# Value products of an attention kernel put into other slots, and transposes put ahead of scores

## The reference

```python
latent_kv = x @ w_kv_down                 # rank 128
kv = latent_kv @ w_kv_up
k, v = kv[..., :HD], kv[..., HD:]         # 16 heads of 64
q = (x @ w_q).reshape(Bx, Tx, N_HEAD, HEAD_SIZE)
att = einsum('bqhd,bkhd->bhqk', q, k) * HEAD_SIZE ** -0.5
att = softmax(where(causal, att, -inf))
y = einsum('bhqk,bkhd->bqhd', att, v).reshape(Bx, Tx, HD)
x = layernorm(x + y @ w_out)
x = layernorm(x + experts(x))             # router, top tokens per expert, gelu
```

## Time and profile before

| | us |
|---|---|
| median of 3 runs | 3311.64 (3307.95 to 3320.35) |
| profiled execution | 3316.82 |
| its span, first to last instruction | 3315.0 |
| busy in the span: TensorE | 2963.1 (89%) |
| VectorE | 2074.8 (63%) |
| ScalarE | 1933.2 (58%) |
| GpSimd | 1578.2 (48%) |

### The profile page before, as it was taken

How to read it: one execution, slowest core, us unless ns; L and a number is a source line. 1 busy time by engine, 2 the same in 40 slices (tenths; PEclk the granted TensorE clock), 3 DMA queues, 4 the chain that set the end, 5 groups by cost and what they waited for, 6 DMA issues and landing times. The chain is left out here.

```text
span 3315.0 us, 65032 instructions
## 1 busy us (share of the span) xinstructions
PE 2963.1 (89%) x20800; PEld 2263.0 (68%) x20800; DVE 2074.8 (63%) x5640; ACT 1933.2 (58%) x4173; POOL 1578.2 (48%) x1661
## 2 busy tenths in 40 slices
PE   7888888888888888888888888888999999999997
PEld 5555555555555555555555555558998999999996
DVE  5665666666666666666666666664596885544546
ACT  5666666666666666666666666664544444444443
POOL 3343334334334333433433343334776776666665
PEclk9999999999999999999999999999999999999998
DMA  2332333333333233233332423335754444443435
GB/s 69 108 109 89 110 106 94 111 104 106 95 101 121 87 101 117 91 115 99 104 104 92 129 84 113 108 106 214 271 209 118 107 122 101 89 113 87 86 72 157
DMA packets 342714, 374.37 MB, mean 113 GB/s; under 512 B 68296, under 2 KB 283080, under 8 KB 342368
## 3 DMA queue, kind: packets, MB, share of 16 engines
q1 hardware_dynamic: 300320, 319.62, 30.4%
q0 software_dynamic: 25152, 33.75, 6.1%
q10 hardware_dynamic: 16896, 16.78, 1.4%
HBM read 211.85 MB, written 158.16 MB: 112 GB/s over the span
## 5 line engine op out<-in xcount | busy, mean ns | idle before, releaser
L270 POOL TENSOR_SCALAR prob<-prob,inv 128x128 f32<-128x128 f32 (+7 forms) x1024 | 756.7, 750 | 1229.7 <-DVE inv L710 734.6
L705 DVE CUSTOM_DVE_ANT_0 s_ps<-s_ps,mask 128x128 f32<-128x128 f32 (+7 forms) x1024 | 757.0, 779 | 345.4 <-PE s_ps L411 338.6
L592 ACT ACTIVATE prob<-s_ps,neg_max 128x128 f32<-128x128 f32 (+7 forms) x1024 | 754.7, 740 | 282.3 <-DVE neg_max L705 278.6
L428 PE MATMUL t_ps<-ident,prob 128*128 128x128 f32 x3328 | 528.9, 284 | 1.5 <-ACT tri L686 0.9
L686 ACT ACTIVATE prob_t<-t_ps 128x512 f32<-128x512 f32 x512 | 305.2, 596 | 383.0 <-PE t_ps L428 383.0
L428 PEld LDWEIGHTS t_ps<-ident,prob 128*128 128x128 f32 x3328 | 368.7, 141 | 187.8 <-POOL prob L270 74.9
L411 PE MATMUL s_ps<-w_lo,w_hi 64*128 64x512 f32 (+3 forms) x2304 | 277.2, 363 | 144.7 <-ACT prob L592 144.7
L411 PE MATMUL s_ps<-k_of,q_of 64*128 64x512 f32 (+3 forms) x2304 | 277.8, 364 | 133.2 <-ACT prob L592 133.2
L411 PEld LDWEIGHTS s_ps<-w_lo,w_hi 64*128 64x128 f32 x2304 | 188.0, 185 | 221.3 <-ACT prob L592 120.0
L411 PEld LDWEIGHTS s_ps<-k_of,q_of 64*128 64x128 f32 x2304 | 188.4, 186 | 209.4 <-ACT prob L592 113.7
L1771 PE MATMUL e_y<-w_hi,hid_hi 128*128 128x256 f32 (+1 forms) x1088 | 311.9, 287 | 0.0
(11 more groups left out here) (266 smaller groups left out, 6002.1 us busy)
## 6 DMA issues: line engine op xcount, KB each, us to landing
y_d<-c_res SPq DMA_DIRECT2D x128, 256.0 KB, 2.4
s_d<-squares SPq DMA_DIRECT2D x63, 512.0 KB, 3.0
late_t<-s_d SPq DMA_DIRECT2D x252, 128.0 KB, 3.3
c_yt<-y_d SPq DMA_DIRECT2D x60, 512.0 KB, 6.7
s_d<-squares SPq DMA_DIRECT2D x63, 384.0 KB, 2.6
late_t<-s_d SPq DMA_DIRECT2D x252, 96.0 KB, 2.9
b_xt<-w SPq DMA_DIRECT2D x16, 1024.0 KB, 5.1
w_raw<-w SPq DMA_DIRECT2D x16, 1024.0 KB
```

The costliest lines, as they stand in the source:

```text
L270: pool.tensor_scalar(pr, pr, inv[:, s % PB:s % PB + 1], 1.0, ALU.mult, ALU.mult).then_inc(norm_done, 1)
L428: mm = pe.transpose(t_ps[s % 2][:, to * P:(to + 1) * P], prob[s % PB][:, j * P:(j + 1) * P], ident[:])
L592: act.activation(prob[s % PB][:, 0:(q + 1) * P], score_part(s), ACT.Exp, scale=-1.0, bias=neg_max[:, s % PB:s % PB + 1], accum_out=total[: ...
L705: dve.tensor_tensor_reduce(part, part, mask[:, T - (q + 1) * P:T], 1.0, -MASKED, ALU.add, ALU.min, neg_max[:, s % PB:s % PB + 1]).then_inc ...
```

## The change

The tables of the value products are rewritten, and the call `turn(n, s)` stands ahead of the scores of its slot instead of behind them. The value products of the first half stood in slot 13, now tile 0 stands in slot 10 and tiles 1 to 3 in slot 12. Those of the last pair's second half stood in slots 1 (tiles 0 to 3) and 7 (tiles 4 to 7), now in 2 (tiles 0 and 1), 5 (tiles 2 and 3) and 7 (tiles 4 to 7).

```diff
-            values_0 = {13: [0, 1, 2, 3]}
-            values_1 = {1: [0, 1, 2, 3], 7: [4, 5, 6, 7]}
+            values_0 = {10: [0], 12: [1, 2, 3]}
+            values_1 = {2: [0, 1], 5: [2, 3], 7: [4, 5, 6, 7]}
...
                 for s in range(8 * g, 8 * g + 8):
+                    turn(n, s)
                     q = SCORES_AT.get(s, 0)
...
                         scores(n + 1, 1 - u, q - 8)
-                    turn(n, s)
                     if latents(n, m, s) is not None:
```

## The result

The changed kernel takes 3271.48 us (median of 4 runs, 3269.12 to 3272.9), the kernel before, measured beside it, 3315.99 us. The ratio is 0.9867, with a 95% interval from 0.9843 to 0.9892: 44 us or 1.3% faster. The forecast was 3222, 90 us under its own median before. The direction was right and the range (3160 to 3300) held, but the gain was half of the forecast, and the forecast's own range (3180 to 3270) was just missed.

The account below looks back on a forecast made before the run. TensorE's instruction stream, in program order, was taken as the bound. Gains of 82 us (48 ordinary pairs) and 10 (seven pairs behind latents), less about 2 in the last pair, net 90: 3311.6 - 90 = 3222 us, range 3160 to 3300.

Parts of the forecast that it names:

- What bounds it: Attention stage: TensorE's instruction stream in program order sets the pace, working 29.62 of 34.12 us per pair of heads.
- the three old waits: TensorE, ahead of scores of blocks 5, 7 and next pair's 0: waits for exponentials of 1.22, 1.66, 1.62 us.
- The new waits of Q1 and K0: Lower part of a pair: queries' second and keys' first projection wait 0.9 and 0.7 us for VectorE's splits.
- Rival 1: More gain, chance 0.13: new waits in the lower part don't bind, pair about 30.0 us, 3090 us; halfway, 3150.
- The price of a border: TensorE, three more borders per pair between products and other work: taken as 0, at most 0.75 us a pair.
- the walk: One ordinary pair followed instruction by instruction on TensorE: lower part 11.3, upper 21.1, together 32.4 against 34.12 us.
- T5's wait: Lower part, ahead of block 4's scores: step 5's transposes wait 0.4 to 0.5 us for VectorE's copy.
- The pairs with latents gain nothing: Every eighth pair, seven in all: loses 1.8 us behind the first queries' projection, gains nothing in all, counted 0.
- those behind them: The seven pairs after those with latents: six matmuls partly cover the queries' wait, gain 1.4 us each, 10 in all.
- (b): TensorE: transposes of steps 5, 7, 9, 11, 13 fill waits ahead of scores, 0.45 us per four transposes.
- Rival 3: Slower, chance 0.09: clock falls in ordinary pairs, 3.2 us each; in every pair, 94 us lost, 3405 us.
- rival 2: No change, chance 0.09: lower part shrinks only 0.65 us, which the upper part's 0.65 takes away, 3312 us.

Follow-up runs that it names:

- the cover for K0: Products moved, transposes behind scores, tiles 1 to 3 ahead of queries' projection in latents pairs; against that, second half's tiles 0 and 1 back in slot 1: 3188.53 us.
- cut in place: Kernel before, with the second half's first four product tiles cut in two, tiles 2 and 3 moved from slot 1 to slot 2: 3357.41 us, ratio 1.0119.
- the fastest kernel: Against the kernel with tiles 0 and 1 back in slot 1, the queries' second projection moved behind slot 0's scores: 3182.97 us, ratio 0.9601.

## Where the prediction was right and where it failed

- **What bounds it, and the three old waits:** right. In the changed kernel 267 us of waits for exponentials shrink to 31.

```profile
PE s_ps L411 <- ACT prob L592: 31.0, 62, 0.5
PE j_ps L510 <- DVE q_of L722: 22.2, 31, 0.7
```

- **The new waits of Q1 and K0:** right, place and cause. Forecast 0.9 and 0.7 us, measured 0.54 and 0.72; K0 came within 0.05 us of its forecast place. Rival 1 (they don't bind) is answered by these waits, and by the cover for K0, which gave 31 us more.
- **The price of a border, "I take 0":** this step failed first, and it made the ordinary pair 32.97 us instead of 32.4. One cut in place costs 0.31 us. In the changed pair, start to start, the price shows where the walk had none: K0 and K1 cost 0.86 and 0.89 us with products behind them (taken at 0.8), each half of the products 1.87 (1.79), T6 and T7 1.02 (0.9), and from T3 to S4, T5's wait within, pass 1.49 us where 1.2 was forecast. I had argued from starts that follow one another without a gap, but the cost is not a gap. The prediction's own row showed part of it: four transposes cost 0.59 us with products behind them and 0.43 to 0.47 with more transposes behind, and it took 0.45 everywhere.
- **TensorE's busy time** rose by 1.28 us per pair, of which not all is the price of borders. Counted start to start without the waits, over the ordinary pairs, the transposes rose from 6.54 to 7.61 us, the products from 8.19 to 8.50, the projections fell by 0.12 and the scores stayed; with the products alone moved, busy time is 30.52. Part of the rise is how a wait is counted: T2 cost 0.20 us with K0 right behind it, and now counts 0.44 (1006.79 to 1007.95, less the wait of 0.72), since its whole duration passes before the wait begins. With Q1, K0 and T5 three waits begin behind transposes that had none; at some 0.2 us each this is 0.6 to 0.7 of the 1.28, an estimate from these rows. So the three waits held TensorE longer than the 0.54, 0.72 and 0.28 that the profile gives them, nearer to what was forecast.
- **What the failed steps are worth.** By the profiled spans the gain is 47.7 us, and 90 were forecast. The ordinary pairs gave 61 instead of 82 (48 x 0.57 = 27 less, and 5 more since three falls of the clock went), the pairs with latents -20 instead of 0, those behind them 7.6 instead of 10.
- **"The pairs with latents gain nothing":** this step failed second. Each lost 2.8 us on the mean, 20 us in all. The sum set 1.8 us of products and transposes behind Q0's wait against a gain of 1.7 elsewhere; the 1.8 was there (S7 to S0' 9.8 us without a fall, forecast 9.6). Missing were 0.6 us of the ordinary pair's shortfall, 0.85 us of longer lower part where T5 waits 1.09 us for GpSimd, which in these pairs also splits the input, and the clock fall: 1.6 us in five of the seven. The prediction had put up to 22 us for falls (3.2 each) into a paragraph of its own and left it out of the sum; they cost 8. With the transposes of step 5 behind S4, as with the products alone moved, T5's wait isn't there.
- **(b), transposes ahead of the scores, as a filler of waits:** wrong in sign. Alone it costs 32 us, and taken out of the changed kernel it gives 37; some 15 and 12 of these are lower clock. There was no wait ahead of S4 and S6 before, so T5 and T9 had none to fill. And it ties a scores call, which feeds all other engines, to two more engines' progress (T7 to a copy on VectorE, T5 to GpSimd).
- **Rival 3, falls of the clock in ordinary pairs:** not there; the 48 pairs all last 32.95 to 33.01 us. In the kernels that keep the two waits of 1.6 us before S7 and S0', falls do come, in 3, 7 and 11 ordinary pairs. Why in so many of one kernel and so few of another stays open.
- **That the range held was luck in part:** it reached to 3300 for the sake of rival 2, in which K0 would wait so long that nothing is gained. K0 didn't (7.55 us after S0'); the time came near that end by the two steps above, for which the prediction had priced no such sum.

## What to carry to other kernels

When work is moved from a full stretch of an engine into its waits, price the cut as well as the move: here one cut of a block of matmuls cost 0.31 us though no gap shows. And when idle time falls, look at whether busy time rose: 2.42 us less idle time made the pair only 1.14 us shorter. Before you put work ahead of an instruction that feeds other engines, list what that work itself waits for in every variant of the loop, the rare ones too. And when moved work was the cover of another wait, leave just enough behind: two tiles in their old slot, instead of none, gave 31 us.

## What the runs showed of the hardware

- A block of eight calls of 512 columns (16 matmuls in the trace) costs 3.58 us in a row and 2 x 1.87 us in two pieces, and the projection ahead of a piece 0.1 us more than ahead of a transpose.
- After a wait of 2.50 us TensorE's granted clock was 0.68 over the next 5.3 us in five of seven cases; after one of 1.06 us in none of seven, though two of the seven pairs behind them had a later fall. After one of 2.11 us in front of the same Q0 it fell in one of seven in the kernel before and in four of seven with the products moved alone (37.8 us instead of 36.2).
- A change of 0.3 us in a loop of 34 us took the number of clock falls in ordinary pairs from 3 to 11 of 48, with the same waits. Nothing that I read in the rows tells how many there will be.
- Summed over the attention stage, (1 - granted clock) x length is 15.4 us in the kernel before, 18.8 in the changed one, 6.8 with the products alone, 30.7 with the transposes alone, 34.1 with the cut in place and 0 in the fastest kernel. These are estimates from the granted clocks. Between two orders of the same work this can be as large as what the order itself gives: the clock is to be read beside every difference.
